# First attention: value sums of both head sets in one PSUM bank, three banks for the products that VectorE reads, waits block by block

## The reference, cut to what matters

```
qkv = x @ w_qkv.T;  q, k, v = split into 16 heads of 8 columns;  q, k = rope(q), rope(k)
scores = causal(q @ k.T / sqrt(8));  attn = softmax(scores);  out = (attn @ v) @ w_out.T
x1 = layernorm(x + out)
h = silu((x1 @ w1.T) * s1) * ((x1 @ w2.T) * s2)          # 128 -> 512
h = gelu((h @ h1.T) * s_h1);  h = gelu((h @ h2.T) * s_h2)  # 512 -> 512 -> 512
x2 = layernorm(x1 + (h @ w3.T) * s3)                      # 512 -> 128
```

## Time and profile before

| | us |
|---|---|
| median of 3 runs | 3275.83 (3272.88 to 3276.35) |
| the profiled execution, its own time | 3288.68 |
| its span, first to last instruction | 3286.9 |
| mean granted TensorE clock over the span | 0.911 |
| TensorE matmul busy over the span | 2715.9 (83%) |
| VectorE busy | 2309.8 (70%) |
| ScalarE busy | 2086.8 (63%) |
| GpSimd busy | 1239.6 (38%) |

### The profile page before, as it was taken

The page is one execution under the profiler, slowest core; times in us unless marked ns, Lnnn a source line. Parts: engine busy times, 40 slices in busy tenths (PEclk is TensorE's granted clock), DMA queues, the critical chain, the costliest instruction groups (busy, mean ns, idle before and its releaser), DMA issues. The chain is left out here.

```text
span 3286.9 us, 59887 instructions
## 1 busy us (share of the span) xinstructions
PE 2715.9 (83%) x18884; PEld 1634.5 (50%) x18884; DVE 2309.8 (70%) x7740; ACT 2086.8 (63%) x5457; POOL 1239.6 (38%) x3658
## 2 busy tenths in 40 slices
PE   3678888888888888888888888888888888876898
PEld 1234333333333456555555555556556556555565
DVE  3445355444423399899799799899799888887465
ACT  0244655555453588788788788787787787874331
POOL 2111011101000256555565565565565565674000
PEclk6678889989889799999899999999999999987899
DMA  2111011001010211211211211211211211221342
GB/s 91 34 36 37 8 37 40 23 19 40 5 45 10 46 32 37 54 33 36 52 37 32 53 39 31 57 36 28 60 37 25 59 39 24 57 47 40 92 98 65
DMA packets 111295, 137.13 MB, mean 42 GB/s; under 512 B 20448, under 2 KB 90592, under 8 KB 110464
## 3 DMA queue, kind: packets, MB, share of 16 engines
q1 hardware_dynamic: 110976, 133.25, 17.8%
HBM read 47.62 MB, written 13.24 MB: 19 GB/s over the span
## 5 line engine op out<-in xcount | busy, mean ns | idle before, releaser
L1242 ACT ACTIVATE junk<-xs,thr 128x420 bf16<-128x420 f32 (+12 forms) x832 | 466.0, 570 | 74.8 <-POOL thr L957 59.8
L1083 PE MATMUL pt<-wsc,attn 128*128 128x128 f32 x2560 | 364.1, 292 | 101.9 <-POOL wsc L938 65.4
L1070 PE MATMUL pm<-mixin,pre_b 128*128 128x258 f32 (+15 forms) x1088 | 371.2, 457 | 91.2 <-ACT xs L1235 80.9
L1083 PEld LDWEIGHTS pt<-wsc,attn 128*128 128x128 f32 x2560 | 325.9, 200 | 192.7 <-POOL wsc L938 132.8
L615 DVE TENSOR_REDUCE row_max<-po 128x1 f32<-128x384 f32 (+3 forms) x352 | 209.5, 637 | 290.8 <-PE po L457 289.8
L1364 DVE MAX8 best<-left 128x8 f32<-128x420 f32 (+12 forms) x832 | 368.4, 483 | 0.0
L1036 PE MATMUL pa<-kT,qT 64*128 64x258 f32 (+3 forms) x1280 | 290.7, 457 | 85.6 <-ACT arena L1204 62.2
L1204 ACT ACTIVATE arena<-pa,nrm 128x258 f32<-128x258 f32 (+3 forms) x640 | 273.4, 477 | 105.1 <-PE pa L1036 99.4
L1394 DVE SCALAR_TENSOR_TENSOR attn<-xs,bound,ex 128x420 f32<-128x420 f32 (+14 forms) x480 | 226.6, 500 | 124.8 <-issue 62.0
L1070 PEld LDWEIGHTS pm<-mixin,pre_b 128*128 128x128 f32 x1088 | 179.9, 203 | 228.3 <-issue 198.0
L1261 ACT COPY at<-pt 128x128 f32<-128x128 f32 (+3 forms) x512 | 198.4, 450 | 114.7 <-PE po L1121 97.2
(11 more groups left out here) (235 smaller groups left out, 5960.8 us busy)
## 6 DMA issues: line engine op xcount, KB each, us to landing
spread<-gates_dram SPq DMA_DIRECT2D x32, 512.0 KB, 7.9
mixin<-arena SPq DMA_DIRECT2D x32, 258.0 KB
mixin<-arena SPq DMA_DIRECT2D x32, 242.0 KB
mixin<-arena SPq DMA_DIRECT2D x32, 226.0 KB
mixin<-arena SPq DMA_DIRECT2D x32, 210.0 KB
mixin<-arena SPq DMA_DIRECT2D x32, 194.0 KB
parts_dram<-parts SPq DMA_DIRECT2D x16, 384.0 KB, 3.9
q_stack<-parts_dram SPq DMA_DIRECT2D x96, 64.0 KB
```

The source lines that it names most:

```text
L1070: ins = nc.tensor.matmul(bank[:, 0:jn], pre_b[:, :], mixin[:, m % MIX_SLOTS, j0:j0 + jn], start=True, stop=not last)
L1083: ins = nc.tensor.matmul(bank[:, P * k:P * k + P], attn[:, m % A_SLOTS, P * k:P * k + P], wsc[:, m % A_SLOTS], start=True, stop=True)
L1242: ins = nc.scalar.activation(junk[:, z, 0:width(n)], xs[:, m % X_SLOTS, 0:width(n)], ACT.Sign, scale=-1.0, bias=thr[:, s % LIVE, z:z + 1], ...
```

## The change

- The third bank: ring `O` has three banks, `psum["o"]` and the first of `psum["t"]`; `o_bank` waits for the product three places back.
- The value sums of both sets share the other bank of `psum["t"]`. The first chunk of each set's sums waits until VectorE has copied out the sums of the set before it.
- Waits block by block: in h1:0 and h2:0 matmul j waits for input block j, in y1 and y0 the same within the first output tile.
- `TURN` moves out of the function with the same strings. The condition for `h2` in `plan` becomes `n >= TT`; h2 stands in chunks 0, 1 and 7 only, so the order stays the same.

```diff
-        banks_c, banks_o, banks_t = psum["a"] + psum["m"], psum["o"], psum["t"]
+        banks_c, banks_o, av_bank = psum["a"] + psum["m"], psum["o"] + psum["t"][:1], psum["t"][1]
...
-                    out += there("h2", b - (1 if n == CHUNKS - 1 else 2), int(arg[0]), arg[1:])
+                    out += there("h2", b - (1 if n >= TT else 2), int(arg[0]), arg[1:])
...
-        C, O = Ring(C_KEYS, 4), Ring(O_KEYS)
+        C, O = Ring(C_KEYS, 4), Ring(O_KEYS, 3)
...
                 def o_bank(key):
-                    if O.nth(key) > 2:
-                        pe.wait_ge(o_free, O.nth(key) - 2)
+                    if O.nth(key) > 3:
+                        pe.wait_ge(o_free, O.nth(key) - 3)
                     return banks_o[O.bank(key)]
...
                 def values(b, n):
-                    if b and k == 0:
-                        pe.wait_ge(sums_done, 2 * (b - 1) + g + 1)
+                    if k == 0 and 2 * b + g:
+                        pe.wait_ge(sums_done, 2 * b + g)
...
-                            ins = nc.tensor.matmul(banks_t[g][at:at + 2 * SUM_COLS, P * k:S],
+                            ins = nc.tensor.matmul(av_bank[at:at + 2 * SUM_COLS, P * k:S],
...
                 def project(b):
-                    pe.wait_ge(out0_done, 2 * (b + 1))
...
+                            if t == 0:
+                                pe.wait_ge(out0_done, 2 * b + g + 1)
...
                 def hidden_1(b, k, part):
-                    if k == 0 and part != "b":
-                        pe.wait_ge(o_free, O.nth(("f2", b, KC - 1)))
...
+                        if k == 0:
+                            pe.wait_ge(o_free, O.nth(("f2", b, j)))
...
                 def hidden_2(b, k, part):
-                    if k == 0 and part != "b":
-                        pe.wait_ge(c_free, C.nth(("h1", b, KC - 1)))
...
+                        if k == 0:
+                            pe.wait_ge(c_free, C.nth(("h1", b, j)))
...
                 def down(b):
-                    pe.wait_ge(c_free, C.nth(("h2", b, KC - 1)))
...
+                            if t == 0:
+                                pe.wait_ge(c_free, C.nth(("h2", b, j)))
...
-                    nc.vector.tensor_copy(sums_in[:, g], banks_t[g][:, :]).then_inc(sums_done, 1)
+                    nc.vector.tensor_copy(sums_in[:, g], av_bank[:, :]).then_inc(sums_done, 1)
```

More of the change, by code:

```diff
@@ L166, in rows @@
     return bank[:, :].rearrange("p (t d) -> p t d", t=TT)
+TURN = ("v R C R C V S1 R h2:2a R h2:2b C start:0 C R",
[7 rows of a table added]
 def first_phase(nc, psum, d, x2_d, parts_d, maxes_d, arena, wts2, x2_0):
@@ L218, in first_phase @@
                 for g in range(SETS)]
-        TURN = ("v R C R C V S1 R h2:2a R h2:2b C start:0 C R",
[7 rows of a table removed]
         BACK = dict(y0=1, x1=1, x1T=1, f=1, h1=1, y1=2, x2=2)
```

## The result

The changed kernel takes 3180.01 us (median of four runs, 3177.41 to 3185.67) against 3276.09 us: a ratio of 0.9713, 95% interval 0.9698 to 0.9728. That is 96 us less, where 73 were forecast, and just outside the range given (3183 to 3230). The direction and the place were right. The time is near that of rival (b), 3185 us, which had a chance of 0.2.

A forecast was written before the change was run, and what follows sets the result against it. PE was taken to bound the first phase. Batches 2 to 6 give 44 us, batch 1 9, batch 7 8, round 8 2.4, the start 10: 73 us off 3275.8, so 3203 us, range 3183 to 3230.

The forecast's parts named there:

- rival (b): First phase: with the 4.5 us pause cut to 1.7, slow clock spells go too; 17 us more, 3185 us; chance 0.2.
- PE bounds the repeated batches: One first-phase batch: PE is busy for 98.32 of 116.1 us, and its named waits account for 17.7 of 17.8 us lost.
- The third bank: Repeated batch: R waits for one bank's read, not both; 4.8 of 7.6 us of bank waits go.
- The conversion named: Behind y1: the last savings turn into a longer wait before mT, so f:0 comes 3.3 us earlier, not 4.
- h1:0, 4.0 us a batch: After f:3: h1:0 starts block by block and ends 3.9 to 4.4 us earlier; 4.0 taken, its wait falling to about 1.7.
- Nothing for h2:0, y1, y0 in the repeated batches: Block-by-block waits there give nothing for eight batches; 2.4 us in the last round, h1:0 included.
- no cost of the shared bank: Value sums of a set: the added wait for VectorE's copy has 8.3 and 11.9 us in hand; cost 0.
- The sum: First phase: 8.8 us per steady batch, 73 us in total, so a median of 3203 us.
- the 10 forecast: Batch 0 and the eleven R before it: 20 row-max waits give up to 0.5 us each, 10 us taken.
- The signs of being wrong: Repeated batch: L440's waits rise as L453's fall, L476 waits for L636, or mean clock moves over 0.03 from 0.90.

The follow-up runs named there:

- e1_bank: The kernel before with the third bank and the shared bank for value sums alone, waits on whole stages kept; 3209.1 us, ratio 0.9784.
- e2_waits: The kernel before with the block-by-block waits alone (h1:0, h2:0, y1, y0); 3241.8 us, ratio 0.9884.
- e4_h1only: The kernel before with the block-by-block waits in h1:0 alone; 3243.9 us, ratio 0.9899.
- e3_share: The kernel before with both sets' value sums in one bank, ring O left at two banks; 3278.1 us, ratio 0.9999.
- e9_once: The changed kernel with three 512-column matmuls of no use ahead of y1 in one batch alone; 3185.7 us, ratio 0.9717.
- e12_padbefore: The kernel before with one 512-column matmul of no use ahead of y1 in every batch; 3289.0 us, ratio 1.0032.
- e10_again: The changed kernel run once more, nothing altered; 3186.4 us, ratio 0.9719 against the kernel before.
- e5_warm: The kernel before with four 512-column matmuls of no use ahead of the wait of h1:0, no wait removed; 3261.8 us, ratio 0.9942.

## Why the prediction was wrong, point by point

- *PE bounds the repeated batches, and nearly all of its idle time there has a name (17.7 of 17.8 us).* Right.
- *The third bank, 4.8 us a batch.* Right in its waits: 4.5 alone (e1_bank). The conversion named, savings behind y1 turning into mT's wait, is there: 0.7 to 1.3.
- *h1:0, 4.0 us a batch.* Its idle part was right at 2.7 (e2_waits). Of its busy part I had 5.40 going to about 4.05, and it went to 3.97: also right, for this one group.
- *Nothing for h2:0, y1, y0 in the repeated batches, no cost of the shared bank.* Right (e4_h1only, e3_share).
- *The sum.* This is the step that failed. It let the granted clock change the time of h1:0 alone and left every other matmul at its old duration. Per repeated batch it had 7.45 us of idle time (8.8 less the 1.35 of h1:0's slow records) and 1.35 of busy time; measured were 7.5 and 2.6 in batches 3 to 6, and in batch 2 busy time fell by 8.2 (98.3 to 90.2). Over the first phase the sum had some 64 us of idle time (73 less 7 x 1.35) and got 57; it had 9 of busy time and got 39. So the term that was mis-sized is the clock's, by 30 us, and the idle term was 7 too large. The forecast missed by only 23 because the two errors have opposite signs.
- Where the 7 went: 3.5 in the stretch up to batch 1, 1.5 in batch 1, 0.5 in batch 2, 1.8 behind batch 6; batches 3 to 6 gave 0.6 more than forecast. In the first stretch the waits of R fell by 11.5 us (22.9 to 11.4), more than the 10 forecast, but PE then waited longer for the load-back of the maxima (21.9 us and not 16.9 in DMA waits before C), so 6.5 were left.
- *Rival (b), the clock stays up,* priced at 17 us more. The clock is what it said, the way to it is not. In batches 3 to 6 the mean clock is 0.90 as before: the shorter batch has nearly as large a slow share, 20.5 of 105.9 us against 23.9 of 116.1. Only batches 0 to 2 and the last ones run at a higher clock, and they have 28.6 of the 38.8 us. I tied the rival to pauses that get shorter, but a batch of e9_once waits no less than one of the changed kernel (10.7 and 10.2 us) and has half of its slow time (10.2 and 20.5 us). The account that fits is that the slow spells of a batch also depend on where it falls against the clock's changes, and that a batch hands its position on to the next; that part is inferred. That (b)'s total of 3185 us came near is in part luck, since it kept the idle term that was 7 too large.
- The signs of being wrong: a batch's clock that moves by more than 0.03 from 0.90 was one. Batch 2 at 0.97 shows it; batches 3 to 6 do not.
- The range was too narrow for this: its upper gain should have had the slow time of all matmuls in it, not of h1:0 and a spell or two.

What stays open: which length the batches of a given run take, and how much of the medians of e9_once and e12_padbefore comes from their first phases and how much from the later ones. A profile shows one execution, and timed runs list no batches. What makes the clock fall in a batch whose longest wait is 1.8 us is not shown either.

## What to carry to other kernels

Where an in-order PE bounds a stretch, add up its waits by name, and follow a removed wait to where it returns; that forecast 7.45 us a batch here, and 7.5 went. Then price the slow clock apart, as half of PE's busy time at the low level, over the whole stretch and not at the removed wait alone; take it as a term with both signs and with a spread of its own. Low clock that falls on a pause costs nothing, so work that only moves can gain or lose. And judge a small edit of such a kernel by more than one variant: in one profile a matmul of no use added 0.9 us of work and took 3.5 us off a batch, which the timed runs neither confirm nor refute.

## What the runs showed that I had not expected

- A repeated batch can stay at one length to 0.1 us while 0.9 us of work is added to each (116.1 us in the kernel before and in e12_padbefore), and two lengths can alternate (105.0 and 110.1 us in e1_bank, 109.2 and 112.7 in e2_waits).
- Nearly the same waits and the same instructions took 105.9 us a batch, or 102.5 after one delay of 2.7 us (e10_again, e9_once).
- Filling a wait with four matmuls of no use made the kernel before 0.58% faster (e5_warm).
